# Exact fp32 weight products rewritten as three float32r products in a graph-block kernel

## The reference, cut to what matters

```
idx = top_k(-d2, 8)
for i in range(4):
    p = where(points >= 0, points, 0.01 * points)
    g = take_along_axis(p, idx)
    c = einsum('oi,bin->bon', w[i], p)
    gn = einsum('oi,bikn->bokn', w[i], g)
    points = (c + gn.sum(axis=2)) / 9 + shortcut
```

## Time and profile before

| | |
|---|---|
| Time, median of 3 executions | 356.79 us (356.51 to 357.43) |
| Profiled execution: span from first to last instruction | 355.5 us |
| Median time less that span | 1.3 us |
| PE busy | 348.0 us, 98% |
| PE weight loads busy | 273.1 us, 77% |
| DVE busy | 197.9 us, 56% |
| ACT busy | 57.2 us, 16% |
| POOL busy | 2.3 us, 1% |

### The profile page before, as it was taken

The page is one execution under the profiler, slowest core; times in us unless marked ns, Lnnn a source line. Parts: engine busy times, 40 slices in busy tenths (PEclk is TensorE's granted clock), DMA queues, the critical chain, the costliest instruction groups (busy, mean ns, idle before and its releaser), DMA issues.

```text
span 355.5 us, 4129 instructions
## 1 busy us (share of the span) xinstructions
PE 348.0 (98%) x1560; PEld 273.1 (77%) x1560; DVE 197.9 (56%) x340; ACT 57.2 (16%) x97; POOL 2.3 (1%) x11
## 2 busy tenths in 40 slices
PE   4999999999999999999999999999999999999997
PEld 1667666666666788888888888888888888888886
DVE  0138384377357379855556555655565556555654
ACT  1111112021111231222111111111111111111110
POOL 2000000000000000000000000000000000000000
PEclk9999999999999999999999999999999999999999
DMA  7994433433210000000000000000000000000113
GB/s 237 344 341 171 148 118 120 148 118 118 79 68 0 0 0 2 0 0 2 1 0 0 0 0 0 0 0 0 0 0 0 0 0 0 0 0 0 59 59 118
DMA packets 7478, 20.01 MB, mean 56 GB/s; under 512 B 688, under 2 KB 1968, under 8 KB 6448
## 3 DMA queue, kind: packets, MB, share of 16 engines
q1 hardware_dynamic: 7472, 19.93, 16.7%
HBM read 17.83 MB, written 2.10 MB: 56 GB/s over the span
## 4 chain that ended last, share of the span: by engine, by line
PE 97%; DMA 2%; SPq 0%; DVE 0%; issue 0%
PE bank L268 33%; PE bank L256 31%; PE bank L196 29%; DMA points<-in_ctx_dram 2%; PE bank L203 1%; PE bank L246 1%; PE bank L215 0%; PE bank L231 0%; PE bank L235 0%; PE bank L223 0%; PE bank L222 0%; SPq L143 0%; DVE state L460 0%
## 5 line engine op out<-in xcount | busy, mean ns | idle before, releaser
L256 PE MATMUL bank<-w_t,relu 128*128 (+1 forms) x512 | 115.8, 379 | 0.0
L196 PE MATMUL bank<-points 128*128 128x512 f32 (+3 forms) x384 | 109.5, 439 | 4.9 <-DMA points<-in_ctx_dram 4.9
L256 PEld LDWEIGHTS bank<-w_t,relu 128*128 128x128 f32 x512 | 96.9, 190 | 14.0
L268 PE MATMUL bank<-adj,y_hi 128*128 128x512 f32 (+1 forms) x260 | 105.9, 409 | 0.0
L268 PE MATMUL bank<-adj,y_lo 128*128 128x512 f32 (+1 forms) x260 | 100.1, 386 | 0.0
L196 PEld LDWEIGHTS bank<-points 128*128 128x128 f32 x384 | 65.3, 192 | 39.3 <-issue 19.2
L460 DVE SCALAR_TENSOR_TENSOR state<-bank,state 128x512 f32<-128x512 f32 (+1 forms) x65 | 44.1, 682 | 46.6 <-PE bank L268 46.6
L451 DVE TENSOR_TENSOR y_lo<-bank,y_hi 128x512 fp32r<-128x512 f32 x64 | 44.2, 691 | 43.8 <-ACT y_hi L363 43.7
L363 ACT CAST y_hi<-bank 128x512 fp32r<-128x512 f32 x64 | 37.6, 587 | 183.1 <-PE bank L256 183.1
L268 PEld LDWEIGHTS bank<-adj,y_lo 128*128 128x128 f32 x260 | 48.9, 188 | 9.6
L268 PEld LDWEIGHTS bank<-adj,y_hi 128*128 128x128 f32 x260 | 48.9, 188 | 9.7
(11 more groups left out here) (39 smaller groups left out, 64.9 us busy)
## 6 DMA issues: line engine op xcount, KB each, us to landing
points<-in_ctx_dram SPq DMA_DIRECT2D x8, 1024.0 KB, 5.7
points<-in_ctx_dram SPq DMA_DIRECT2D x8, 256.0 KB, 3.0
points<-in_ctx_dram SPq DMA_DIRECT2D x4, 512.0 KB, 5.6
state<-in_x_dram SPq DMA_DIRECT2D x4, 512.0 KB, 13.7
out_dram<-state SPq DMA_DIRECT2D x7, 256.0 KB, 2.0
rest<-in_ctx_dram SPq DMA_DIRECT2D x8, 128.0 KB, 5.1
w_raw<-in_fside_BxSxS_dram SPq DMA_DIRECT2D x1, 1024.0 KB, 13.4
last_row<-in_ctx_dram SPq DMA_DIRECT2D x1, 1024.0 KB, 17.9
```

The costliest lines, as they stand in the source:

```text
L196: mm = nc.tensor.matmul(bank[i][:, 0:N - i * P], points[:, t, i * P:(i + 1) * P], points[:, t, i * P:N], start=(t == 0), stop=False)
L256: mm = nc.tensor.matmul(dst, relu[:, b, h, q * P:(q + 1) * P], w_t[:, w, h, :], start=(h == 0), stop=(h == CH - 1))
L268: mm = nc.tensor.matmul(bank[to][:, cols], part[:, b % 2, q, h * P:(h + 1) * P], adj[:, b, q, cols], start=(q == 0 and part is y_hi), stop ...
```

## The change

The weight product is formed from three float32r products. With h = (1 - 2^-13) x rounded to float32r, l = x - h (as float32r) and m = h - 4096 l for both factors (the weights' low part carries the factor 4096), y is the sum of h·h and l·4096l, less m·m/4097, and the common factor 1 + 1/4096 goes into the ninth (`SHARE`). `y_step` is now 4 + 8 matmuls per half of the points, 24 in all, each float32r and 256 columns wide. The high and low products go to banks 0 and 2, the mixed ones to banks 1 and 3, so Y has one set of banks, not two, and waits for `y_ready` of the step before.

Around it: ACT makes the leaky relu (`Prelu`) and its high part (`relu_high`, L431, L433), POOL the low part (`relu_low`, L211), DVE the mixed part (`relu_mixed`, L494). `relu` is one buffer for all batches, so ACT waits for POOL's low part of the relu before. Of y, ACT scales the mixed product out of its bank (`y_mixed`, L441), DVE adds the other bank (`y_sum`, L570), ACT rounds (`y_high`, L447), and the low part is split: POOL takes half 0 (L217), DVE half 1 (L575). The weights get three parts too (L453, L459, L501, L507). `y`, `y_hi` and `y_lo` lie where `points` lay, so Y(0) waits for the gram rows of the last batch; `marked` is replaced by `gram`. All loops are written out.

Core of the diff:

```diff
-            def y_step(s, w, b):
-
-                pe.wait_ge(relu_ready, s + 1)
-                for q in range(NB):
-                    dst = bank[Y_BANKS[b % 2][q // 2]][:, (q % 2) * C:(q % 2 + 1) * C]
-                    for h in range(CH):
-                        mm = nc.tensor.matmul(dst, relu[:, b, h, q * P:(q + 1) * P], w_t[:, w, h, :],
-                                              start=(h == 0), stop=(h == CH - 1))
-                    if q % 2:
-                        mm.then_inc(y_done, 1)
+            def y_step(s, w, b, first=False):
+
+                pe.wait_ge(r_mixed_ready, s + 1)
+                for g in range(2):
+                    if not first:
+                        pe.wait_ge(y_ready, 2 * s + g - 1)
+                    for q in (2 * g, 2 * g + 1):
+                        dst = bank[MIXED_BANKS[g]][:, (q % 2) * C:(q % 2 + 1) * C]
+                        for h in range(CH):
+                            mm = nc.tensor.matmul(dst, r_mixed[:, b, h, q * P:(q + 1) * P], w_mixed[:, w, h, :],
+                                                  start=(h == 0), stop=(h == CH - 1))
+                    mm.then_inc(mixed_done, 1)
+                    for q in (2 * g, 2 * g + 1):
+                        dst = bank[MAIN_BANKS[g]][:, (q % 2) * C:(q % 2 + 1) * C]
+                        for h in range(CH):
+                            nc.tensor.matmul(dst, r_high[:, b, h, q * P:(q + 1) * P], w_high[:, w, h, :],
+                                             start=(h == 0), stop=False)
+                            mm = nc.tensor.matmul(dst, r_low[:, b, h, q * P:(q + 1) * P], w_low[:, w, h, :],
+                                                  start=False, stop=(h == CH - 1))
+                    mm.then_inc(main_done, 1)
...
+            pe.wait_ge(w_mixed_ready, BLOCKS)
+            pe.wait_ge(gram_ready, B * NB)
+            y_step(0, 0, 0, first=True)
...
+            def relu_high(n, b, ready=None):
+
+                if ready is None:
+                    act.wait_ge(state_ready, 2 * n - 2 * B + 2)
+                else:
+                    act.wait_ge(ready, 16)
+                if ready is None or n > 0:
+                    act.wait_ge(r_low_ready, n)
+                nc.scalar.activation(relu[:, :, :], state[:, b, :, :], ACT.Prelu, alpha=SLOPE).then_inc(relu_ready, 1)
+                act.wait_ge(relu_ready, n + 1)
+                nc.scalar.mul(r_high[:, b, :, :], relu[:, :, :], LEAN).then_inc(r_high_ready, 1)
...
+            def relu_low(n, b):
+
+                pool.wait_ge(r_high_ready, n + 1)
+                nc.gpsimd.tensor_tensor(r_low[:, b, :, :], relu[:, :, :], r_high[:, b, :, :].bitcast(fp32),
+                                        ALU.subtract).then_inc(r_low_ready, 1)
...
+            for l in range(BLOCKS):
+                weights(l)
+            for l in range(BLOCKS):
+                weights_mixed(l)
             for b in range(B):
-                dve.wait_ge(x_in[b], 16)
-                make_relu(b)
+                relu_mixed(b, b)
             dve.wait_ge(last_col_ready, B * NB)
...
-                    y_low(l * B + b, b)
-                    update_and_relu(l * B + b - 1, (b - 1) % B, OUT[(b - 1) % 2])
+                    s = l * B + b
+                    y_sum(s)
+                    update(s - 1, (b - 1) % B, OUT[(b - 1) % 2], slice(0, 1))
+                    y_low(s, b, 1)
+                    relu_mixed(s + B - 2, (b - 2) % B)
+                    update(s - 1, (b - 1) % B, OUT[(b - 1) % 2], slice(1, 2))
```

More of the change, by code:

```diff
@@ L45, in knn_blocks_kernel @@
     TAKEN = -3.4028234663852886e38
+    SHIFT = 4096.0
+    LEAN = 1.0 - 2.0 ** -13
+    UNMIX = -1.0 / (SHIFT + 1.0)
+    SHARE = (1.0 + 1.0 / SHIFT) / (K + 1)
     CHUNKS = [range(0, 4), range(4, 8), range(8, KT)]
@@ L157, in _ @@
                 sp.dma_start(state[:, b, :, :], x[b, :, :].rearrange("(h p) n -> p h n", p=P)).then_inc(x_in[b], 16)
-            with sp.Fori(1, B) as b:
+            for b in range(1, B):
                 for n, (_, _, chunk) in enumerate(LOADS):
@@ L286, in _ @@
                 gram_rows(0, 2, i, first_batch=True)
-            with pe.Fori(0, B - 1) as before:
+            for before in range(0, B - 1):
                 for i in range(2):
@@ L320, in _ @@
             turn_neighbours(B - 1)
-            with pe.Fori(1, LAYERS) as l:
+            for l in range(1, LAYERS):
                 for b in range(B):
@@ L369, in _ @@
                 act.wait_ge(w_turned, l + 1)
-                nc.scalar.copy(w_t[:, l, :, :], bank[6 + l % 2][:, :].rearrange("p (h o) -> p h o", h=CH))\
-                    .then_inc(w_ready, 1)
-            with act.Fori(0, B - 1) as b:
+                nc.scalar.mul(w_high[:, l, :, :], bank[6 + l % 2][:, :].rearrange("p (h o) -> p h o", h=CH), LEAN)\
+                    .then_inc(w_high_ready, 1)
+            for b in range(B):
+                relu_high(b, b, ready=x_in[b])
+            for l in range(BLOCKS):
+                act.wait_ge(w_rest_ready, l + 1)
+                nc.scalar.mul(w_low[:, l, :, :], w_raw[:, l, :, :], SHIFT).then_inc(w_ready, 1)
+            for b in range(0, B - 1):
                 rest_high(b + 1)
@@ L438, in neighbours @@
                 dve.drain()
-                nc.vector.match_replace(marked[:, i, :], top8[:, i, :], dist[:, i, :], TAKEN).then_inc(marked_ready, 1)
+                nc.vector.match_replace(gram[:, i, :], top8[:, i, :], dist[:, i, :], TAKEN).then_inc(marked_ready, 1)
                 if i < NB - 1:
@@ L459, in update @@
+            def update(s, b, pieces, which=slice(None)):
+                for n, (h, cols, at) in tuple(enumerate(pieces))[which]:
                     dve.wait_ge(out_done, 2 * s + n + 1)
-                    nc.vector.scalar_tensor_tensor(state[:, b, h, cols], bank[at][:, cols], 1.0 / (K + 1),
+                    nc.vector.scalar_tensor_tensor(state[:, b, h, cols], bank[at][:, cols], SHARE,
                                                    state[:, b, h, cols], op0=ALU.mult, op1=ALU.add)\
```

167 lines of the change are left out of this document (123 added, 44 removed).

## The result

The changed kernel takes **410.39 us** (median of 4 executions, 409.64 to 411.16) against 357.11 us (356.51 to 357.68) for the kernel before on the same chip: a ratio of 1.149 [1.147, 1.152]. It is 53 us slower. The forecast was 377.8 us with a range of 369 to 406, so its sign was right and its size wrong: the time lies above the range, 5 us above the 405 of the first rival, the one in which DVE and POOL shut each other out, and 2 us above the 386 to 408 given to that case.

A forecast was written before the change was run, and what follows sets the result against it. PE bounded the kernel before; after the change, a ring of ACT and DVE would set the repeated steps. Span 355.5 + 14.7 + 1.7 + 0.5 + 6.6 - 2.5 = 376.5, plus 1.3 around it: 377.8 us, range 369 to 406.

The forecast's parts named there:

- the first rival: In each step DVE's low part of y waits 1.0 us for POOL's: 8.1 a step, 405 us; chance 0.32.
- the low part at 0.60 in the ring: DVE's low part of y (half 1) was priced at 0.60 us in each step, with no wait for POOL.
- the ring: Waits between ACT (2.66) and DVE (4.44) that close once per step: relu, y, update; 7.1 us a turn.
- Start, +14.7: Before batch 1, PE waits from 35.62 to 50.3 for DVE's gram row, behind four relu rounds of 4.5 us.
- Clock, +1.7: After the start's wait PE may begin at half speed: four records at 0.43 more, 1.7 us, bounds 0 and 3.4.
- Y(0) waits, +0.5: The first weight product, Y(0), waits for all gram rows: 0.5 us.
- Steps 0 to 3, +6.6: From Y(0) to Y(4) DVE becomes the chain: 33.5 us where it was 26.9, so 6.6 more.
- 24 steps at 7.1: Steps 4 to 27 take 7.1 us each, against 7.09 before, and so cost 0.
- The last steps, -2.5: Once the relus end, PE sets the pace at 6.5 us and four steps give back 2.5.
- PE's saving: Y's 24 matmuls at 0.12 us take 2.87 against 3.46: 0.59 less per step, 6.5 a step if PE bounds.
- POOL's price: POOL's subtraction taken at 2.3 us for 1024 elements and 1.2 for 512; bounds for 1024 were 0.96 and 2.34.
- Faster, at 0.05: Rival: ACT and DVE run the ring in less than 6.5 us, PE stays the bound; 349.5 us, chance 0.05.

The follow-up runs named there:

- the three orders together: Changed kernel with DVE's low part before POOL's, the start's mixed relus behind the neighbours, and the second update piece before the mixed relu; 359.53 us, ratio 1.005.
- the last kernel: The one ahead of it, with both low parts of y on DVE and POOL keeping only the relu's low part; 348.10 us, ratio 0.973.
- the one ahead of it: The three orders together, with ACT's and DVE's start reordered and, in steps 0 to 3, updates and next y moved earlier; 351.51 us, ratio 0.980.

## Why the prediction was wrong, and where it was right

**The step that failed: the low part at 0.60 in the ring.** The forecast took DVE's low part at its duration alone and gave 0.6 to that case, though the rival beside it had the mechanism, the place (DVE reaches its low part 2.5 us after the high part, while POOL's runs from 2.34 to 3.5) and the price (1.0 a step). In the trace DVE's L575 starts 2.48 after POOL's L211 and takes 1.69, not 0.69: 1.0 more in nearly all of the 24 steps, and the step is 8.17, not 7.1. "No row speaks for or against, since POOL is idle" was true, and then the rule of the Trainium skill (SBUF — State Buffer, § Who interferes with whom) was the only evidence there was; the forecast put it at a third. The runs bear it out: the wait goes when POOL only writes, changes sides when DVE comes first, and goes when POOL has no part in y.

**The rival's 405 was 5 us short** for the terms beside it:
- *Start, +14.7.* Measured +15.6. The round of 4.5 us took 4.66 (the relus start at 35.29, 39.95, 44.60), with 1.06 for relu and high part each and 2.34 for POOL's 1024. The first round took 4.92, its 1024 at POOL 2.59.
- *Clock, +1.7.* Measured 9.03 less 6.23, 2.8, within its bounds. The windows of the changed kernel, behind the wait of 15.6:

```profile
51.23:54.50 3.27, 3.27 (x4) 1.48 (x5) 3.10 (x13) 0.00 (x0) 0.00 (x0) 0.50 0.00 0
54.50:57.50 3.00, 3.00 (x5) 1.20 (x4) 1.58 (x3) 0.00 (x0) 0.00 (x0) 0.61 0.00 0
57.50:60.30 2.80, 2.80 (x10) 1.71 (x9) 0.00 (x0) 0.00 (x0) 0.00 (x0) 1.00 0.00 0
```

  (stretch, its length, busy time of PE, PEld, DVE, ACT and POOL, then the granted clock.) It stood at 0.50, 1.2 GHz, for the first 3.27 us and at 2.4 from 57.5 on.
- *Y(0) waits, +0.5.* Measured 0.64. So Y(0) came 19.2 later, where 16.9 was given.
- *Steps 0 to 3, +6.6.* Measured +10.0. The work was counted right, but POOL's low parts stretched DVE's here too: the four took 0.82, 1.29, 1.71 and 1.70, 2.8 more than 4 x 0.69. The rest is half a microsecond; with POOL's memset, where none of the four is stretched, the stretch takes 34.1, given as 33.5.
- *24 steps at 7.1.* Without the collision they are 7.18, so the ring's sum was right to 0.1, and the two prices that were estimates held: relu with the leaky function 1.06 where 1.045 was taken, the high part 1.06. With it they are 8.17. That is 24 x 1.07 = 25.7 on this term. *The last steps, -2.5*: by the marks Y(4) to the end grew by 24.2, so 1.5 of the 2.5 came.

In sum: 1.0 more for stall and wait, 1.1 for the clock, 3.4 in the first steps, 25.7 in the loop and 1.0 at the end are 32.2, against 32.3 between the span of 408.8 and the 376.5 forecast for it. (The 0.3 that is left up to the 32.6 between the times lies outside the span.)

**The bounds of the forecast** were looser than their reasons. For the range of 369 to 386 without shutting out, the terms named give 370.7 (5.4 less for a cheap POOL, 1.7 less for the clock) and about 382 (24 x 0.1 for ACT and 1.7 for the clock); the rest had no row behind it.

**What was right.** PE's saving: the 24 matmuls of Y stand 0.12 apart, and where PE is the bound a step takes 6.58, given as 6.5; there Y takes 2.86 and O 3.72, where 2.87 and 3.63 were given. That it would be gained and waited away: even without the collision a step is 7.18 against 7.09 before. In the changed kernel PE waits 30.9 us for L570. That the mixed relus would stop batch 1 at the gram row. Loops at nothing. POOL's price: 2.38 and 1.29, close to what the upper of its two bounds gives, the one from an instruction that reads.

**Faster, at 0.05**, asked that the ring be 0.6 shorter than its rows. As written it is not; with the wait beside POOL and the mixed relu both out of it, it is.

## What to carry to other kernels

When work is moved off a bound engine, write down the ring of waits that one step then closes and add it up: what stands in the ring costs in full, what stands beside it costs nothing, and moving an instruction out of it (a few lines of order) was worth 27 us here, more than the arithmetic saved. Give no work to GpSimd that reads SBUF at the time when VectorE has an instruction with two SBUF inputs on that ring; if it must, let VectorE come first. After each stall that is mended, look for the next one in the same queue before counting the gain.

## What the runs showed of the hardware

- DVE and POOL instructions with two SBUF inputs didn't run side by side at their own pace in any row that was read: DVE's 0.69 became 1.68 to 1.73 in 23 of the 28 steps from Y(4) on, its 0.29 became 1.99, POOL's 1.29 became 2.14. With the three orders together they still meet (DVE's mixed relu takes 1.45, not 1.21), but off the ring. A memset on POOL (0.53) beside the same DVE instruction cost it nothing. DVE's sums and updates, with one input in PSUM, kept 0.68 to 0.69 beside POOL.
- A DVE instruction that was shut out ended 0.55 after POOL's end, less than its own 0.69.
- Waits of under 3 us were followed by a granted clock near the lower level (0.50, 1.2 GHz) in two kernels. In the last kernel PE waited 2.89 us for the last neighbours, after two shorter waits; the four matmuls that take 0.63 to 0.71 took 1.00, and the granted clock from 153.82 to 157.50 was 0.54. In the one ahead of it, the 2.55 us waited up to 146.77 were followed by 0.60 for 4.2 us, and the 1.69 waited up to 154.00 by 1.00. In the kernel before the change, which never waited there, it stayed at 1.00. The length of the wait doesn't settle it: in the kernel with three orders, 3.14 us waited up to 155.29 were followed by 1.00 for 2.7 us.
